# The last sum of a router layer: added by two turns into PSUM instead of by VectorE

## The chip, the cores and the metric

The kernel runs on one NeuronCore of one Trainium2 chip. The core has five engines that run side by side and wait for each other by semaphores: TensorE (PE; its weight loads are shown apart as PEld), VectorE (DVE), ScalarE (ACT), GpSimd (POOL) and SyncE (SP), which issues DMAs. The metric is device time in microseconds (us) of one execution. All arithmetic is float32.

## The reference

A small tower over 32 images of 257 tokens with 256 features. Layer 0 is a Mamba block of four scans and a mixture of experts, layer 1 is attention and a routed feed-forward. What matters here is the very last function and its last line:

```python
def _L1_ffn_ref(x, attention_mask, wr, br, w1, b1, w2, b2):
    weights = (jnp.einsum('bsd,do->bso', x, wr) + br)[..., 0]
    _, idx = jax.lax.top_k(weights, k)
    sel_idx = idx[:, :kk]
    sel = jnp.take_along_axis(x, sel_idx[:, :, None], axis=1)
    h = jax.nn.gelu(jnp.einsum('bkd,dh->bkh', sel, w1) + b1)
    y = jnp.einsum('bkh,hd->bkd', h, w2) + b2
    y = y * w_sel[..., None]
    processed = jnp.zeros_like(x).at[batch_idx, sel_idx].set(y)
    return processed + x
# layer 1, last step
h = h + _L1_ffn_ref(_layernorm(h, axis=-1), ...)
```

So the output is the sum of three terms: h, its layer norm x, and `processed`, which is y times the router's weight for a kept token and zero for the others.

## The kernel before

There are two phases with a barrier between them. `mamba_phase` does layer 0's Mamba part for all images and leaves the result in DRAM (`h_mid`). `tail_phase` does everything else. The change touches `tail_phase` alone.

`tail_phase` takes the images two at a time, in 16 groups. Features lie on the 128 partitions in two chunks (`CM = 2`), and tokens in the free dimension, so a tile such as `xh` is [128, 2 chunks, 2 images, 257 tokens]. The work of one group is cut into three stages: F (experts), A (attention) and R (router, feed-forward, output). The stages form a pipeline: in turn t, F works on group t, A on group t-1 and R on group t-2. Turns 0, 1 and 2 are written out, turns 3 to 15 are a hardware loop (waits there compare with registers), and turns 16 and 17 are written out again: turn 16 has A and R only, turn 17 has R only.

The order inside a turn is a table written by hand, `turn_order` (line 997). Each name in it is a slot: TensorE fills the PSUM banks of its stage (`ps["R"]` has two banks), another engine reads them out, and the next slot of the same stage waits for that reading by the counter `read[s]`. Each engine walks the same table, and does what it has to do in each slot. The end of the table is:

```python
A.score_1 R.hid_6 F.e1_2 R.hid_7 F.e1_3 A.turned_0 F.s2 R.y_0 F.gates_t A.turned_1 F.e2_0 R.y_1 F.e2_1 A.mix_0
F.gates_0 R.out_0 A.mix_1 R.out_1 F.gates_1
```

The slots that matter are these.

- `R.var` (line 1410): VectorE makes x, and then `xh` = x + h (line 1416).
- `R.y_0`, `R.y_1` (lines 1491 to 1499): for each chunk of features TensorE computes the second product into `ps_R` (line 1528). VectorE adds the bias and multiplies by the selected weight into `sq["R"]` (line 1495), and then adds that to `xh` (line 1499), which counts `o_ready`.
- `R.out_0`, `R.out_1` (lines 1623 to 1630): for each image TensorE turns `xh` from features on partitions to tokens on partitions. These are six transposes (three tiles of 86, 86 and 85 tokens by two chunks of features) into different columns of the two banks. ScalarE copies the result to `o_sb` (lines 1329 and 1330), and SyncE stores it with three DMAs (line 1183).
- `R.mean` of the next turn is the next user of `ps_R` after `R.out_1`.

A float32 matrix product is two MATMUL records in the trace, a transpose is one.

`sq["R"]` is written in `R.mean` by ScalarE (line 1259) and in `R.y` by VectorE. The next turn's `R.mean` stands behind `R.out_1` on TensorE.

Of the kernel before, what the change touches and what calls it, by code (L numbers as in the profile page):

```python
# [5 lines left out]
ALU = mybir.AluOpType  # L6
# [3 lines left out]
P = 128  # L10
# [5 lines left out]
CM = DM // P  # L16
# [972 lines left out]
def tail_phase(nc, a, h_mid, out):  # L989
# [26 lines left out]
    with ExitStack() as ctx:  # L1016
# [3 lines left out]
        def sem(name):  # L1020
            return ctx.enter_context(nc.semaphore(name))
# [94 lines left out]
        ahead_part = sem("ahead_part")  # L1116
        ahead_ready = sem("ahead_ready")
        xh_ready = sem("xh_ready")
        o_ready = sem("o_ready")
        stored = [sem(f"stored_{b}") for b in range(NB)]  # L1120

        n_loads = 2 * NE + 21
# [212 lines left out]
        def _(dve):  # L1335
# [62 lines left out]
            def slot(s, name, g):  # L1398
                kind, _, i = name.partition("_")
                if kind == "mean":  # L1400
                    dve.wait_ge(full[s], nth(s, name, g))
                    w = ps[s]
                    for c in range(CM):
                        last = dve.tensor_tensor(x[s][:, c, :, :], h[s][:, c, :, :], w[:, 0:NB, 0:S], ALU.subtract)
                    last.then_inc(read[s], 1)

                    dve.wait_ge(squared[s], g + 1)
                    dve.tensor_tensor(sq[s][:, 0, :, :], sq[s][:, 0, :, :], sq[s][:, 1, :, :], ALU.add
                                      ).then_inc(squares_summed[s], 1)
                elif kind == "var":  # L1410
                    norm(s, g)
                    if s == "R":

                        dve.wait_ge(x_ready[s], g + 1)
                        for c in range(CM):
                            last = dve.tensor_tensor(xh[:, c, :, :], x[s][:, c, :, :], h[s][:, c, :, :], ALU.add)
                        last.then_inc(xh_ready, 1)
                elif (s, name) == ("F", "logits"):
                    route_logits(g)
                elif (s, name) == ("F", "e1_0"):  # L1420
                    route_ranks(g)
                elif (s, name) == ("F", "e1_2"):
                    route_gates(g)
                elif (s, kind) == ("F", "gates") and i != "t":
                    dve.wait_ge(full[s], nth(s, name, g))
                    w = ps[s]
                    dve.tensor_tensor(e2[:, int(i), :, :], e2[:, int(i), :, :], w[:, 0:NB, 0:S], ALU.mult).then_inc(read[s], 1)
                elif (s, kind) == ("F", "out"):
                    c = int(i)
                    dve.wait_ge(full[s], nth(s, name, g))  # L1430
                    w = ps[s]
                    if c == 0:

                        if positive(nth("A", "mix_1", g - 1)):
                            dve.wait_ge(read["A"], nth("A", "mix_1", g - 1))
                    dve.scalar_tensor_tensor(out=h["A"][:, c, :, :], in0=w[:, 0:NB, 0:S], scalar=s_b3[:, c:c + 1],
                                             in1=h["F"][:, c, :, :], op0=ALU.add, op1=ALU.add).then_inc(read[s], 1)
                    if c == CM - 1:

                        dve.wait_ge(read[s], nth(s, name, g))  # L1440
                        sum_stream("A")
                elif (s, kind) == ("A", "score"):
                    b = int(i)
                    dve.wait_ge(full[s], nth(s, name, g))
                    w = ps[s]
                    dve.tensor_reduce(nmax[0:QT, b, 0:2], w[0:QT, 0:2, 0:S], AX.X, ALU.max, negate=True).then_inc(max_ready, 1)
                    dve.tensor_reduce(nmax[0:85, b, 2:3], w[0:85, 2, 0:S], AX.X, ALU.max, negate=True).then_inc(max_ready, 1)

                    dve.wait_ge(read[s], nth(s, name, g))
                    dve.reciprocal(precip[0:QT, b, 0:2], psums[0:QT, b, 0:2])  # L1450
                    dve.reciprocal(precip[0:85, b, 2:3], psums[0:85, b, 2:3]).then_inc(recips_ready, 1)
                    dve.wait_ge(recips_ready, g * NB + b + 1)
                    for q, (t0, n) in enumerate(TILES):
                        last = dve.tensor_scalar(prob[0:n, b, q, :], prob[0:n, b, q, :], precip[0:n, b, q:q + 1], DM ** -0.5,
                                                 ALU.mult, ALU.mult)
                    last.then_inc(probs_ready, 1)
                elif (s, kind) == ("A", "mix"):
                    b = int(i)
                    dve.wait_ge(full[s], nth(s, name, g))
                    w = ps[s]  # L1460
                    if b == 0:

                        if positive(g):
                            dve.wait_ge(xh_ready, g)
                    dve.tensor_tensor(h["R"][:, :, b, :], h["A"][:, :, b, :], w[:, 0:CM, 0:S], ALU.add).then_inc(read[s], 1)
                    if b == NB - 1:

                        dve.wait_ge(read[s], nth(s, name, g))
                        sum_stream("R")
                elif (s, name) == ("R", "hid_1"):  # L1470

                    dve.wait_ge(read[s], nth(s, "column", g))
                    for b in range(NB):
                        for t, (t0, n) in enumerate(TILES):
                            last = dve.scalar_tensor_tensor(out=ahead[0:n, b, t, :], in0=w_rows[0:n, b, :],
                                                            scalar=w_col[0:n, b, t:t + 1], in1=before[0:n, t, :],
                                                            op0=ALU.is_equal, op1=ALU.mult)
                    last.then_inc(ahead_part, 1)
                    dve.wait_ge(ahead_part, g + 1)
                    for b in range(NB):  # L1480
                        for t, (t0, n) in enumerate(TILES):
                            last = dve.scalar_tensor_tensor(out=ahead[0:n, b, t, :], in0=w_rows[0:n, b, :],
                                                            scalar=w_col[0:n, b, t:t + 1], in1=ahead[0:n, b, t, :],
                                                            op0=ALU.is_lt, op1=ALU.add)
                    last.then_inc(ahead_ready, 1)
                elif (s, name) == ("R", "rank"):
                    dve.wait_ge(full[s], nth(s, name, g))
                    w = ps[s]
                    dve.scalar_tensor_tensor(out=sel_w[:, :, :], in0=w[:, 0:NB, 0:S], scalar=float(KEPT), in1=w_rows[:, :, :],
                                             op0=ALU.is_lt, op1=ALU.mult).then_inc(read[s], 1)  # L1490
                elif (s, kind) == ("R", "y"):
                    c = int(i)
                    dve.wait_ge(full[s], nth(s, name, g))
                    w = ps[s]
                    dve.scalar_tensor_tensor(out=sq["R"][:, c, :, :], in0=w[:, 0:NB, 0:S], scalar=b_2[:, c:c + 1],  # L1495
                                             in1=sel_w[:, :, :], op0=ALU.add, op1=ALU.mult).then_inc(read[s], 1)

                    dve.wait_ge(read[s], nth(s, name, g))
                    dve.tensor_tensor(xh[:, c, :, :], xh[:, c, :, :], sq["R"][:, c, :, :], ALU.add).then_inc(o_ready, 1)

            run(dve, lambda turn: walk(turn, slot), lambda: dve.wait_ge(loaded, 16 * n_loads), lambda: None)

        @block.tensor
        def _(pe):
# [12 lines left out]
            def slot(s, name, g):  # L1517
# [86 lines left out]
                else:  # L1604
# [15 lines left out]
                    elif kind == "y":  # L1620
                        cols = slice(int(i) * P, (int(i) + 1) * P)
                        last = product(lambda b: [(w_2[:, k, cols], hid[:, k, b, :]) for k in range(HC)])
                    elif kind == "out":
                        b = int(i)
                        pe.wait_ge(o_ready, g * CM + CM)
                        flat = w[:, :, :].rearrange("p b n -> p (b n)")
                        for t, (t0, n) in enumerate(TILES):
                            for c in range(CM):
                                last = pe.matmul(flat[0:n, t * DM + c * P:t * DM + (c + 1) * P], xh[:, c, b, t0:t0 + n],  # L1629
                                                 ident[:, :], is_transpose=True, start=True, stop=True)  # L1630
                last.then_inc(full[s], 1)

            run(pe, lambda turn: walk(turn, slot), setup, lambda: None)
# [28 lines left out]
```

## Time and profile before

| | |
|---|---|
| time, median of 3 runs | 11963.23 us (11961.89 to 11964.04) |
| the profiled execution's own time | 11969.22 us |
| its span, first to last instruction | 11967.6 us |
| TensorE busy over the span | 9996.1 us, 84% |
| VectorE busy | 10589.7 us, 88% |
| ScalarE busy | 6724.8 us, 56% |
| mean granted TensorE clock | 0.921 of full speed |

The Mamba phase fills the first 10.2 ms or so of the span, and `tail_phase` the rest. Shares over the whole span say little about the second, which has limits of its own; it has to be read in its own stretch.

A row of the page's strips is 40 equal slices of the span, a digit being the busy tenths of a slice. A row of a stretch gives its length, and for each engine the busy time and the number of instructions in it, then the granted clock of TensorE as a share of full speed. A row of the timeline gives start, duration, engine, line, operation, output<-inputs, shapes and count, and in brackets how long the engine had been idle and who ended that. Neighbouring records of one kind are merged into one row; a matmul's record lasts from its issue to its modelled end, and overlaps the next one's. PEclk is 1.0 at 2.4 GHz and 0.5 at 1.2 GHz.

### The profile page before, as it was taken

What the parts mean: (1) busy time and instruction counts of PE and PEld (TensorE: products, weight loads), DVE (VectorE), ACT (ScalarE), POOL (GpSimd) and SP (SyncE); (2) the same over time, 40 slices, a digit from 0 to 9 for tenths busy, and PEclk for the clock granted to TensorE, in tenths of its full rate; (3) what the DMA queues carried; (4) which work ended last, traced back from release to release, by engine and by line L of the source; (5) the groups of instructions that cost most, each with busy time, mean ns of one, the idle gap of its engine ahead of it and who ended that gap; (6) DMA issues with size and microseconds to landing.
All of it is one profiled execution on the core that took longest, in us unless ns stands there. A gap on an engine that the chain in (4) does not pass through costs nothing. (4 is left out here: it accounts for less than half of the span.)

```text
span 11967.6 us, 119737 instructions
## 1 busy us (share of the span) xinstructions
PE 9996.1 (84%) x40728; PEld 7833.4 (65%) x40728; DVE 10589.7 (88%) x8817; ACT 6724.8 (56%) x10429; POOL 94.9 (1%) x167
## 2 busy tenths in 40 slices
PE   6888888888888888888888888888888887799998
PEld 5666666666666666666666666666666665577776
DVE  6999999999999999999999999999999999333332
ACT  5555555555656565555555555565565555244443
POOL 0000000000000000000000000000000000000000
PEclk8999999999999999999999989898999998899998
DMA  2211222222222122222221112222222111000000
GB/s 79 76 62 59 69 76 71 71 72 69 74 68 67 57 75 71 76 71 72 69 76 64 59 67 76 71 72 71 69 74 71 64 60 58 22 11 11 11 11 9
DMA packets 357681, 728.03 MB, mean 61 GB/s; under 512 B 143670, under 2 KB 188890, under 8 KB 357082
## 3 DMA queue, kind: packets, MB, share of 16 engines
q1 hardware_dynamic: 343128, 683.98, 17.1%
q0 software_dynamic: 10240, 33.56, 0.9%
q8 instruction: 328, 5.37, 0.2%
q10 hardware_dynamic: 3714, 2.89, 0.1%
q14 instruction: 271, 2.22, 0.1%
HBM read 699.27 MB, written 21.05 MB: 60 GB/s over the span
## 5 line engine op out<-in xcount | busy, mean ns | idle before, releaser
L892 PE MATMUL y_ps<-hb,ident 128*128 128x257 f32 x16384 | 4506.0, 423 | 1504.8 <-DVE hb L688 1497.9
L892 PEld LDWEIGHTS y_ps<-hb,ident 128*128 128x128 f32 x16384 | 3295.5, 208 | 2533.2 <-DVE hb L688 2022.1
L679 DVE TENSOR_TENSOR_SCAN hb<-decay,hb 128x1028 f32<-128x1028 f32 x2048 | 4722.3, 2306 | 22.4 <-issue 20.8
L505 ACT ACTIVATE decay<-delta,neg_a 128x512 f32<-128x512 f32 x4096 | 2683.0, 712 | 2194.2 <-DVE hb L679 1626.0
L688 DVE TENSOR_TENSOR hb<-hb,c_all 128x1028 f32<-128x1028 f32 x2048 | 2529.8, 1235 | 0.0
L669 DVE TENSOR_TENSOR hb<-b_all,u_buf 128x1028 f32<-128x1028 f32 x2048 | 2496.7, 1219 | 5.8
L783 PE MATMUL w_ps<-xn,in_w 128*128 128x257 f32 x4096 | 1021.8, 396 | 140.6 <-ACT xn L406 115.5
L783 PEld LDWEIGHTS w_ps<-xn,in_w 128*128 128x128 f32 x4096 | 807.7, 199 | 294.8 <-issue 129.6
L783 PE MATMUL w_ps<-xs_pad,diag_store 128*128 128x257 f32 x4096 | 954.8, 379 | 0.2
L783 PEld LDWEIGHTS w_ps<-xs_pad,diag_store 128*128 128x128 f32 x4096 | 774.2, 189 | 114.1 <-ACT diag_store L426 1.0
L783 PE MATMUL w_ps<-sz,out_w 128*128 128x257 f32 x2048 | 513.4, 395 | 0.8 <-DVE sz L696 0.8
L505 ACT ACT_TABLE_LOAD x381 | 488.8, 1283 | 6.7
L437 ACT ACTIVATE xc<-w_ps,conv_b 128x514 f32<-128x514 f32 x256 | 176.4, 689 | 551.2 <-PE w_ps L783 550.0
L783 PEld LDWEIGHTS w_ps<-sz,out_w 128*128 128x128 f32 x2048 | 413.7, 202 | 71.6 <-DVE sz L696 1.5
L783 PE MATMUL w_ps<-dtbc,dt_w 32*128 32x257 f32 x1024 | 353.5, 472 | 3.0 <-ACT cen L456 1.8
L1495 DVE SCALAR_TENSOR_TENSOR sq_R<-ps_R,b,sel_w 128x514 f32<-128x514 f32 x32 | 24.1, 753 | 352.3 <-PE ps_R L1528 352.3
L426 ACT ACTIVATE diag_store<-ident,conv_w 128x128 f32<-128x128 f32 x1024 | 323.9, 390 | 0.0
L888 PE MATMUL y_ps<-xc,skip_diag 128*128 128x257 f32 x1024 | 309.1, 429 | 7.7 <-ACT skip_diag L481 7.7
L424 ACT ACTIVATE xs_pad<-w_ps 128x514 f32<-128x514 f32 x256 | 152.6, 596 | 272.7 <-PE w_ps L783 272.6
L783 PEld LDWEIGHTS w_ps<-dtbc,dt_w 32*128 32x128 f32 x1024 | 205.8, 223 | 146.7 <-issue 117.9
L1528 PE MATMUL ps_R<-x_R,w 128*128 128x257 f32 x1024 | 274.8, 415 | 24.6 <-ACT hid L1321 22.8
L888 PEld LDWEIGHTS y_ps<-xc,skip_diag 128*128 128x128 f32 x1024 | 219.4, 219 | 71.9 <-issue 24.4
(238 smaller groups left out, 9598.5 us busy)
## 6 DMA issues: line engine op xcount, KB each, us to landing
b_all<-bc_dram SPq DMA_DIRECT2D x512, 514.0 KB, 3.6
c_all<-bc_dram SPq DMA_DIRECT2D x512, 514.0 KB, 5.0
in_w<-in_L_attn_in_w SPq DMA_DIRECT2D x64, 1024.0 KB, 5.0
x_in<-in_x POOLq DMA_DIRECT2D x128, 256.0 KB, 2.9
out_w<-in_L_attn_out_w SPq DMA_DIRECT2D x64, 512.0 KB, 3.8
h_mid<-h_cur SPq DMA_DIRECT2D x32, 257.0 KB, 3.4
h_F<-h_mid SPq DMA_DIRECT2D x16, 514.0 KB, 3.7
out<-o_sb SPq DMA_DIRECT2D x64, 86.0 KB
```

What stands on the lines that cost most here:

```text
L424: func(xs_pad[:, c % 2, :, KW - 1:], w[:, :, 0:S], ACT.Identity).then_inc(read_of(f"xs{c}", g, jj), 1)
L426: last = func(conv_diag[:, c % 2, tap, :], ident[:, :], ACT.Identity, scale=conv_w[:, k, c, tap:tap + 1])
L437: func(xc[:, jj % 2, c, :, :], w[:, :, 0:S], ACT.Silu, bias=conv_b[:, k, c:c + 1]).then_inc(read_of(f"cv{c}", g, jj), 1)
L505: last = func(decay[:, u % NDA, i, :, 1:S], delta[:, c, :, 1:S], ACT.Exp, scale=neg_a[:, k, c, NU * n + i:NU * n + i + 1])
L669: dve.tensor_tensor(hb[:, u % NHB, :, :, :].rearrange("p n b s -> p n (b s)"), b_all[:, n, :, :, :].rearrange("p n b s -> p n (b s)"), u_b ...
L679: dve.tensor_tensor_scan(h, decay[:, u % NDA, :, :, :].rearrange("p n b s -> p (n b s)"), h, 0.0, ALU.mult, ALU.add).then_inc(scan_done, 1)
L688: dve.tensor_tensor(h, h, c_all[:, u % PAIRS, :, :, :].rearrange("p n b s -> p (n b s)"), ALU.mult).then_inc(c_done, 1)
L783: last = pe.matmul(w[0:rows, b, 0:S], lhs, rhs, start=(i == 0), stop=(i == len(terms(b)) - 1))
L888: pe.matmul(y_ps[c % 2][:, b, 0:S], skip_diag[:, :], xc[:, jj % 2, c, b, :], start=True, stop=False)
L892: last = pe.matmul(y_ps[c % 2][:, b, 0:S], ident[:, :], hb[:, u % NHB, i, b, :], start=False, stop=(n == PAIRS - 1 and i == NU - 1))
L1495: dve.scalar_tensor_tensor(out=sq["R"][:, c, :, :], in0=w[:, 0:NB, 0:S], scalar=b_2[:, c:c + 1], in1=sel_w[:, :, :], op0=ALU.add, op1=ALU. ...
L1528: last = pe.matmul(w[rows, b, 0:S], lhs, rhs, start=(k == 0), stop=(k == len(terms(b)) - 1))
```

## The change

VectorE no longer adds `sq["R"]` to `xh` in the two `R.y` slots. TensorE instead turns both tiles, each into the same columns of PSUM: the first transpose starts the columns (`start`), the second adds to them (`stop`). So each `R.out` slot has twelve transposes where it had six. TensorE waits for `xh_ready` and for the reading of `y_1` in place of `o_ready`, and that semaphore is gone. Lines below line 1119 move up by one, and later ones by two to four.

```diff
-        o_ready = sem("o_ready")
...
                     dve.scalar_tensor_tensor(out=sq["R"][:, c, :, :], in0=w[:, 0:NB, 0:S], scalar=b_2[:, c:c + 1],
                                              in1=sel_w[:, :, :], op0=ALU.add, op1=ALU.mult).then_inc(read[s], 1)
-
-                    dve.wait_ge(read[s], nth(s, name, g))
-                    dve.tensor_tensor(xh[:, c, :, :], xh[:, c, :, :], sq["R"][:, c, :, :], ALU.add).then_inc(o_ready, 1)
...
                     elif kind == "out":
                         b = int(i)
-                        pe.wait_ge(o_ready, g * CM + CM)
+                        pe.wait_ge(xh_ready, g + 1)
+                        pe.wait_ge(read[s], nth(s, "y_1", g))
                         flat = w[:, :, :].rearrange("p b n -> p (b n)")
                         for t, (t0, n) in enumerate(TILES):
                             for c in range(CM):
-                                last = pe.matmul(flat[0:n, t * DM + c * P:t * DM + (c + 1) * P], xh[:, c, b, t0:t0 + n],
-                                                 ident[:, :], is_transpose=True, start=True, stop=True)
+                                for k, part in enumerate((xh, sq["R"])):
+                                    last = pe.matmul(flat[0:n, t * DM + c * P:t * DM + (c + 1) * P], part[:, c, b, t0:t0 + n],
+                                                     ident[:, :], is_transpose=True, start=(k == 0), stop=(k == 1))
```

On TensorE, in the loop's turn, this stood at `R.out_0` before (`ident` is the unit matrix, `ps_A<-prob_t,value` is `A.mix_1`; a row with x3 stands for three instructions, and brackets name the semaphores waited for):

```order
L1523 REGISTER_ALU
L1625 ISA [waits read_R]
L1629 MATMUL ps_R<-ident,xh 86x128 [waits o_ready]
L1629 MATMUL ps_R<-ident,xh 86x128 x3
L1629 MATMUL ps_R<-ident,xh 85x128 x2
L1523 REGISTER_ALU
L1602 MATMUL ps_A<-prob_t,value 128x257 [waits read_A]
```

and this stands there now:

```order
L1627 MATMUL ps_R<-ident,xh 86x128 [waits read_R,xh_ready]
L1627 MATMUL ps_R<-ident,sq_R 86x128
L1627 MATMUL ps_R<-ident,xh 86x128
L1627 MATMUL ps_R<-ident,sq_R 86x128
L1627 MATMUL ps_R<-ident,xh 86x128
L1627 MATMUL ps_R<-ident,sq_R 86x128
L1627 MATMUL ps_R<-ident,xh 86x128
L1627 MATMUL ps_R<-ident,sq_R 86x128
L1627 MATMUL ps_R<-ident,xh 85x128
L1627 MATMUL ps_R<-ident,sq_R 85x128
L1627 MATMUL ps_R<-ident,xh 85x128
L1627 MATMUL ps_R<-ident,sq_R 85x128
```

Twelve transposes stand where six did, and the separate waiting instruction ahead of them is gone; the slots ahead and behind are the same.

On VectorE, in the same turn, the two `R.y` slots were these (`ps_R` is the product, `h_R` belongs to `A.mix_0`):

```order
L1495 SCALAR_TENSOR_TENSOR sq_R<-ps_R,b,sel_w 128x514 [waits full_R]
L1499 TENSOR_TENSOR xh<-xh,sq_R 128x514 [waits read_R]
L1493 REGISTER_ALU
L1495 SCALAR_TENSOR_TENSOR sq_R<-ps_R,b,sel_w 128x514 [waits full_R]
L1499 TENSOR_TENSOR xh<-xh,sq_R 128x514 [waits read_R]
L1459 REGISTER_ALU
L1465 TENSOR_TENSOR h_R<-h_A,ps_A 128x2x257 [waits xh_ready,full_A]
```

and are these now:

```order
L1494 SCALAR_TENSOR_TENSOR sq_R<-ps_R,b,sel_w 128x514 [waits full_R]
L1492 REGISTER_ALU
L1494 SCALAR_TENSOR_TENSOR sq_R<-ps_R,b,sel_w 128x514 [waits full_R]
L1458 REGISTER_ALU
L1464 TENSOR_TENSOR h_R<-h_A,ps_A 128x2x257 [waits xh_ready,full_A]
```

The two additions are gone, and nothing else on VectorE has moved.

## Rows read from the trace of the kernel before

**Rows 1.** The page's strips: busy tenths in 40 slices.

```profile
PE   6888888888888888888888888888888887799998
DVE  6999999999999999999999999999999999333332
```

**Rows 2.** Stretches, from R.mean to R.mean: turns 2 to 15; then turns 12, 11, 14.

```profile
10391.73:11799.88 1408.15, 1327.09 (x6273) 1029.03 (x6273) 453.46 (x1022) 697.87 (x1078) 15.33 (x14) 0.97 0.04 10
11396.31:11495.76 99.45, 93.92 (x449) 72.75 (x449) 32.41 (x73) 49.88 (x77) 1.09 (x1) 0.98 0.04 11
11295.35:11396.31 100.96, 93.92 (x449) 72.76 (x449) 32.38 (x73) 49.91 (x77) 1.09 (x1) 0.98 0.04 10
11595.57:11697.81 102.24, 97.21 (x449) 75.41 (x449) 32.42 (x73) 49.91 (x77) 1.10 (x1) 0.95 0.03 10
```

**Rows 3.** Waits of TensorE behind VectorE's addition: the total, times, the longest.

```profile
PE ps_R L1629 <- DVE xh L1499: 1.7, 1, 1.7
```

**Rows 4.** Timeline of one turn of the loop around R.out_0 and R.out_1.

```profile
11387.11 0.69 DVE L1499 TENSOR_TENSOR xh<-xh,sq_R 128x514 f32<-128x514 f32 x1
...
11391.10 0.85 PE L1629 MATMUL ps_R<-ident,xh 128*86 128x128 f32 x6
...
11391.80 2.77 PE L1602 MATMUL ps_A<-prob_t,value 86*128 86x257 f32 x12
...
11394.41 0.82 PE L1629 MATMUL ps_R<-ident,xh 128*86 128x128 f32 x6
...
11395.16 1.13 PE L1528 MATMUL ps_F<-gate_t,pair_rows 4*128 4x257 f32 x4
...
11395.33 0.70 DVE L1344 TENSOR_TENSOR rstd_R<-h_R 128x514 f32<-128x514 f32 x1
11395.75 0.37 ACT L1330 ACTIVATE o_sb<-ps_R 85x256 f32<-85x256 f32 x1
...
11396.26 1.13 PE L1528 MATMUL ps_R<-rstd_R,mean_w 128*128 128x257 f32 x4
```

**Rows 5.** One line's instructions, nanoseconds min/median/max: the transposes, the addition.

```profile
L1629 PE MATMUL ps_R<-ident,xh x192: 270/273/311, 10487.6 to 11956.6; 128*86 128x128 f32 x128, 128*85 128x128 f32 x64
```

```profile
L1499 DVE TENSOR_TENSOR xh<-xh,sq_R x32: 694/695/697, 10474.0 to 11953.4; 128x514 f32<-128x514 f32 x32
```

**Rows 6.** Timeline of turn 16, which has no gates slots.

```profile
11878.44 0.82 PE L1629 MATMUL ps_R<-ident,xh 128*86 128x128 f32 x6
...
11879.38 2.87 PE L1602 MATMUL ps_A<-prob_t,value 86*128 86x257 f32 x12
...
11883.87 1.14 PE L1528 MATMUL ps_R<-rstd_R,mean_w 128*128 128x257 f32 x4 [0.95 <-ACT o_sb L1330]
```

**Rows 7.** Timeline of the end of turn 17.

```profile
11952.59 0.75 DVE L1495 SCALAR_TENSOR_TENSOR sq_R<-ps_R,b,sel_w 128x514 f32<-128x514 f32 x1 [6.57 <-PE ps_R L1528]
11953.38 0.69 DVE L1499 TENSOR_TENSOR xh<-xh,sq_R 128x514 f32<-128x514 f32 x1
...
11954.22 0.83 PE L1629 MATMUL ps_R<-ident,xh 128*86 128x128 f32 x6 [1.67 <-DVE xh L1499]
...
11955.98 4.98 SPq L1183 DMA_DIRECT2D out<-o_sb  x6
...
11957.39 0.37 ACT L1330 ACTIVATE o_sb<-ps_R 85x256 f32<-85x256 f32 x1
```

**Rows 8.** Timeline of TensorE in turn 17: one form of block at two clocks.

```profile
11910.74 3.79 PE L1528 MATMUL ps_R<-x_R,w 128*128 128x257 f32 x8 [0.78 <-ACT hid L1321]
...
11934.52 2.00 PE L1528 MATMUL ps_R<-x_R,w 128*128 128x257 f32 x8 [0.78 <-ACT hid L1321]
```

**Rows 9.** A stretch with fifteen transposes in it, and the stretch that holds R.column.

```profile
11375.70:11382.00 6.30, 6.30 (x41) 4.92 (x40) 1.45 (x2) 2.15 (x4) 0.00 (x0) 1.00 0.00 0
```

```profile
11416.10:11420.80 4.70, 4.70 (x21) 3.94 (x22) 0.69 (x1) 4.48 (x7) 0.00 (x0) 0.64 0.00 0
```

**Rows 10.** R.column on TensorE, at the start of the second of these stretches.

```profile
11416.09 1.07 PE L1613 MATMUL ps_R<-ones,w_row 1*86 1x1 f32 x12 [1.37 <-ACT hid L1321]
```

## The prediction

> **What bounds the kernel now.** First the page's strips [rows 1]. In the first 33 slices VectorE is at nine tenths and TensorE at eight: that is the Mamba phase, which the change doesn't touch. In the slices that follow it is the other way round, TensorE at seven to nine tenths and VectorE at three, and there the changed code runs. The view of stretches confirms it [rows 2]: turns 2 to 15 take 1408.15 us, in which TensorE is busy for 1327.09 (94%) and VectorE for 453.46 (32%). So the change takes work from an engine that is idle two thirds of the time and gives it to the one that sets the pace.
>
> Next, who waits for the removed addition. The table of waits has one wait of TensorE behind it in the whole phase, 1.7 us [rows 3]. The timeline of a turn of the loop shows why [rows 4]: the addition for `y_1` starts at 11387.11 and lasts 0.69, so it is done at 11387.80, and TensorE reaches `R.out_0` at 11391.10. The addition had 3.3 us of slack, with `A.mix_0` and `F.gates_0` as its cover. Nothing of VectorE's waits in its shadow either: its next instruction waits for `A.mix_0`. So in the loop the removal is worth nothing.
>
> **The cost of a transpose.** The trace has 192 of them, 270 to 311 ns each, median 273 [rows 5], but they overlap, so what counts is the spacing of their starts. `R.out_1`'s block of six is 0.82 us long [rows 4]; less the last one's 0.273 that leaves 0.547 us for five steps, 0.109 us each. `R.out_0`'s block gives (0.85 - 0.273) / 5 = 0.115, since its first step is a little longer; the added ones come behind the first. I take 0.109. As a check, `R.out_0` starts at 11391.10 and `A.mix_1` at 11391.80, 0.70 us for six. The added transposes have the same shapes and the same moving operand, and a stationary one of the same size. What the trace doesn't show is a transpose that adds to PSUM. Bounds for one: 0 from below, if it hid wholly under its neighbour's load, which no row shows; from above 0.217, a step of the neighbouring float32 products (`A.mix_1`, twelve in 11391.80 to 11394.41), were it done as two passes like them. The shapes decide for 0.109.
>
> The Trainium skill, "TensorE: Matmul & The Clock Gate", section "Back-to-back issue gap", gives N/2.4 + 2.5 ns for a single stream at full clock, which is 56 ns for 128 columns; the page's example is bf16. The rows here have twice that for float32, and the measurement decides. By the page's figure the added 192 would cost 10.7 us rather than 20.9.
>
> **The sum at an unchanged clock.**
> - Turns 2 to 15: twelve more transposes each, 12 x 0.109 = 1.31 us. Does anything absorb it? Behind `R.out_0` comes `A.mix_1` without a pause, behind `R.out_1` comes `F.gates_1` without a pause. The next turn's `R.mean` starts at 11396.26, when the last ScalarE copy of `R.out_1` (11395.75 + 0.37 = 11396.12) is done; VectorE's `rstd_R` was there at 11396.03 [rows 4]. The copy moves with the transposes, so that wait stays, and at most 0.1 us a turn is won if it was VectorE's. ScalarE's copy of `R.out_0` has to be done before `R.out_1`; it has the 2.6 us of `A.mix_1` for that, and the added steps shift both alike. 14 x 1.31 = 18.3 us.
> - Turn 16: from `R.out_0` (11878.44) to `A.mix_1` (11879.38) are 0.94 us where six transposes need 0.70; `A.mix_1` waits for VectorE there [rows 6]. So 0.25 of the added 0.65 is hidden, +0.40. `R.mean` then waits for the copy of `R.out_1`, so the other six count in full, +0.65. Together +1.05.
> - Turn 17: here the removal is worth something. TensorE waits for `y_1`'s reading and then for the addition, from 11953.38 to 11954.22 [rows 7]. That goes, about -0.75; late next is the reading itself, done at 11953.34. `R.out_0`'s six added steps (+0.65) make its copy 0.1 us earlier than before. `R.out_1` comes 0.55 later, but its three stores stand in SyncE's queue, which issues six in 4.98 us, 0.83 each: the fourth is due at 11955.98 + 2.49 = 11958.47, and the copy that it needs was done at 11957.39 + 0.37 = 11957.76, now 11958.31. So the end moves by -0.1, at worst by +0.55.
>
> 18.3 + 1.05 - 0.1 = +19.3 us.
>
> **The clock term.** The 14 turns do the same work and don't take the same time. Three kinds stand in the rows [rows 2]: 99.45, 100.96 and 102.24 us. Seven of the 14 are near the first (99.7 in the mean), four near the second (101.0), three near the third (102.1), and the mean of all is 1408.15 / 14 = 100.58. TensorE's own busy time is 93.9 in the first two and 97.2 in the third. The difference is where a stretch at 1.2 GHz falls. The usual place is behind a thin piece, a wait of 1.37 us and the twelve tiny matmuls of `R.column` [rows 10], in a stretch whose granted clock is 0.64 [rows 9]. The cheap kind is half of all turns before. A turn that is 1.31 us longer meets the clock at another point each time, and there is no reason for it to keep the cheap half; I expect the middle kind, 101.0 of before's time. 14 x (101.0 - 100.58) = +5.9 us. Bounds: all cheap, 14 x (99.7 - 100.58) = -12.3; all dear, 14 x (102.1 - 100.58) = +21.3. In turn 17 a block of eight takes 2.00 us at 2.4 GHz and 3.79 at 1.2 [rows 8]; one or two blocks may change sides, +-3.6.
>
> **The total.** The profiled execution had 11969.22 us, 1.6 more than its span of 11967.6, and 6.0 more than the median of 11963.23. Its sum is 11969.2 + 19.3 + 5.9 = 11994.4; against the median 11963.2 + 25.2 = 11988.4, rounded to 11988. A measurement of this kernel tells about 0.2% from no change, 23.9 us, so the line between slower and no change is at 11987.2, right under the forecast.
>
> **The rivals.**
> - *The cheap turns stay as many.* Then only the steady sum is left: 11963.2 + 19.3 = 11982.5, no change. For it: the sequence of turns repeats itself over long stretches, and could do so again. Against: it repeats with a length that the change alters.
> - *Not slower: the stretch at 1.2 GHz always falls cheaply.* The place is `R.column` and the slots behind it. If the longer turn put it there every time, all turns would be 99.7 + 1.3, and the sum 19.3 - 12.3 = +7.0, 11970.2. It decides from a mean turn below 102.2 us (100.58 + 1.31 + 0.33); under that the whole is within 0.2%. Half of before's turns speak for it, the change of phase against it.
> - *Transposes don't hold the clock.* `R.out` with its neighbours now has 24 transposes in 6 us. If the clock fell there, each turn would get a second stretch at half clock, and be of the dear kind: 14 x 1.5 = +21.3 over the mean of before, 11963.2 + 19.3 + 21.3 = 12003.8. Against it: `F.gates_t` and `A.turned_1`, 15 transposes in a row, stand in a stretch with a granted clock of 1.00, and the products behind them too [rows 9]. The same time comes out if the stretches of before just fall at dear places.
> - *The adding transpose takes two passes,* 0.217 in place of 0.109. +20.9 more in 192, 11963.2 + 25.2 + 20.9 = 12009.3. Nothing in the trace speaks for it but the products.
> - *Faster: the freed VectorE lets TensorE go on.* Price: all the waits behind the addition, 1.7 us [rows 3], against 19.3. I don't see it.
>
> The Trainium skill, the same page, section "Part 4: PE-mode transpose", states that transposing doesn't count as TensorE activity for the clock in the way that products do. That is the third rival's rule. By it the sum would be the 12003.8 of that rival; what this case's rows have against it is the 1.00 beside fifteen transposes, which are fewer and shorter together than what comes now.
>
> **How the numbers follow.** The forecast with its clock term has 0.56, with a range of its own from 11984 to 11994; about two thirds of that, 0.38, is over 11987.2. The first rival has 0.20, the second 0.08, the third 0.10, the fourth 0.04, the last 0.02. Slower: 0.38 + 0.10 + 0.04 = 0.52. No change: 0.18 + 0.20 + 0.08 = 0.46. Faster: 0.02. The range from 11977 to 12002 holds the forecast and the first rival whole and what lies halfway to the second and the third; it leaves out about 0.2.
>
> **What would show it.** In the profile after: 384 transposes with a median of 273 ns, blocks of twelve about 1.47 us long, `A.mix_1` 1.35 us behind `R.out_0` and `F.gates_1` 1.40 behind `R.out_1`; no line for the addition, VectorE's busy time in turns 2 to 15 lower by 28 x 0.695 = 19.5 us with no wait of TensorE gone; turns with a mean of 102.3 us, and of the kinds 100.8, 102.3 and 103.5; the last copy of turn 17 at 0.55 later, the end unmoved. A spacing above 0.109, a mean turn below 102.2, or a granted clock under 1.00 around `R.out` would make the forecast wrong, each in its own way.

## The result and the profile after

| | before | changed |
|---|---|---|
| median of 15 runs | 11965.38 us (11958.32 to 11977.47) | 11993.11 us (11982.17 to 12005.43) |
| ratio | | 1.0021, 95% interval 1.0013 to 1.0029 |
| profiled execution, its own time | 11969.22 us | 11994.06 us |
| span | 11967.6 us | 11992.5 us |

The change makes the kernel slower by 0.21%, 25 us, with an interval from 16 to 35; the two medians are 27.7 us apart. The forecast of 11988 against 11963.2 was +24.8, and the profiled span grew by 24.9. More executions of the kernel before moved its median to 11965.4.

The changed kernel's stretches, from R.mean to R.mean, columns as in [rows 2] (turns 2 to 15 together; turns 2, 6 and 12; then turns 16 and 17 from another view):

```profile
10390.08:11825.05 1434.97, 1341.07 (x6440) 1042.98 (x6441) 433.94 (x994) 698.46 (x1078) 15.37 (x14) 0.98 0.03 10
10390.08:10494.01 103.93, 96.80 (x461) 75.04 (x461) 30.79 (x71) 49.89 (x77) 1.10 (x1) 0.97 0.03 7
...
10800.91:10904.45 103.54, 98.52 (x462) 76.66 (x461) 31.04 (x71) 49.93 (x77) 1.10 (x1) 0.95 0.03 10
...
11415.95:11518.24 102.29, 95.23 (x462) 74.08 (x461) 31.01 (x71) 49.91 (x77) 1.10 (x1) 0.98 0.03 10
```

```profile
11825.00:11910.79 85.79, 76.25 (x343) 59.27 (x342) 24.03 (x48) 34.13 (x56) 0.00 (x0) 0.94 0.02 7
11910.79:11992.50 81.71, 52.41 (x196) 37.08 (x196) 11.72 (x22) 15.09 (x23) 0.00 (x0) 0.76 0.04 11
```

Turns 2 to 15 took 1408.15 and now take 1434.97 us. Turns 16 and 17 before were these:

```profile
11799.88:11883.91 84.03, 74.65 (x332) 57.58 (x331) 25.42 (x50) 34.12 (x56) 0.00 (x0) 0.94 0.03 8
11883.91:11967.60 83.69, 53.16 (x184) 36.99 (x184) 13.10 (x24) 15.07 (x23) 0.00 (x0) 0.73 0.04 11
```

In turns 2 to 15 VectorE's busy time fell by 19.5 us, and nothing came of it. TensorE has 12 instructions more a turn (461 where it had 449). And the mix of [rows 2] is gone: 12 of the 14 turns last 102.24 to 102.35 us.

The transposes, minimum/median/maximum in ns:

```profile
L1627 PE MATMUL ps_R<-ident,xh x192: 271/273/311, 10487.5 to 11982.0; 128*86 128x128 f32 x128, 128*85 128x128 f32 x64
...
L1627 PE MATMUL ps_R<-ident,sq_R x192: 270/273/273, 10487.7 to 11982.1; 128*86 128x128 f32 x128, 128*85 128x128 f32 x64
```

Those that add to PSUM (`sq_R`) are as long as those that start the columns. TensorE's timeline in `R.out_0` of a loop turn gives their spacing:

```profile
11409.48 0.31 PE L1627 MATMUL ps_R<-ident,xh 128*86 128x128 f32 x1
11409.63 0.27 PE L1627 MATMUL ps_R<-ident,sq_R 128*86 128x128 f32 x1
11409.74 0.27 PE L1627 MATMUL ps_R<-ident,xh 128*86 128x128 f32 x1
...
11410.72 0.27 PE L1627 MATMUL ps_R<-ident,sq_R 128*85 128x128 f32 x1
11410.83 1.03 PE L1598 MATMUL ps_A<-prob_t,value 86*128 86x257 f32 x4
```

Steps of 0.109 us, and `A.mix_1` starts 1.35 us behind the first transpose, where it was 0.70 in [rows 4]. The stretch around the transposes has a granted clock of 1.00:

```profile
11408.00:11417.00 9.00, 9.00 (x52) 7.15 (x51) 3.46 (x5) 1.73 (x4) 0.00 (x0) 1.00 0.09 25
```

Where the clock does fall shows in TensorE's timeline of turn 12. In the kernel before (99.45 us) it falls in the blocks behind `R.column` (the twelve matmuls of [rows 10]), and `F.logits` (L1551, 24 matmuls with four columns each) and the block behind it run at full clock:

```profile
11417.09 1.79 PE L1528 MATMUL ps_A<-sq_A,mean_w 128*128 128x257 f32 x4
11418.67 2.97 PE L1528 MATMUL ps_R<-x_R,w 128*128 128x257 f32 x8
...
11423.03 1.97 PE L1528 MATMUL ps_A<-x_A,qk_t 128*128 128x257 f32 x8 [0.52 <-DVE x_A L1339]
...
11443.13 2.74 PE L1551 MATMUL ps_F<-g_w,x_F 128*128 128x4 f32 x24
11445.73 1.98 PE L1528 MATMUL ps_R<-x_R,w 128*128 128x257 f32 x8
```

In the changed kernel (102.29 us) it is the other way round: full clock behind `R.column`, half clock behind `F.logits` (now L1547):

```profile
11436.78 1.14 PE L1524 MATMUL ps_A<-sq_A,mean_w 128*128 128x257 f32 x4
11437.75 1.90 PE L1524 MATMUL ps_R<-x_R,w 128*128 128x257 f32 x8
...
11442.55 1.97 PE L1524 MATMUL ps_A<-x_A,qk_t 128*128 128x257 f32 x8 [2.03 <-DVE x_A L1338]
```

```profile
11462.65 2.74 PE L1547 MATMUL ps_F<-g_w,x_F 128*128 128x4 f32 x24
11465.25 3.12 PE L1524 MATMUL ps_R<-x_R,w 128*128 128x257 f32 x8
11468.16 2.49 PE L1524 MATMUL ps_F<-x_F,e_w 128*128 128x257 f32 x8
```

Before, the blocks behind `R.column` ran at half clock (2.97 us for a block of eight matmul records, 1.90 at full clock). In the changed kernel they run at full clock, and yet `A.key_0` (output `ps_A`, input `qk_t`) starts hardly sooner: 11423.03 - 11396.31 = 26.72 us into the turn before, 11442.55 - 11415.95 = 26.60 now. It waits for VectorE's x_A, 0.52 us before and 2.03 now. So half clock at this place costs 0.1 us: it fills a wait. Behind `F.logits` TensorE waits for nobody, and half clock costs its full price. That place is what the turn of 102.29 us pays for, and the prediction had not seen it.

The trace of the kernel before had it too. In its turn 11, of the middle kind (100.96 us), the one stretch at half clock stands behind `F.logits`:

```profile
11341.99 2.74 PE L1551 MATMUL ps_F<-g_w,x_F 128*128 128x4 f32 x24
11344.59 2.66 PE L1528 MATMUL ps_R<-x_R,w 128*128 128x257 f32 x8
11347.05 2.94 PE L1528 MATMUL ps_F<-x_F,e_w 128*128 128x257 f32 x8
```

By the granted clock of the trace, the seven turns of the cheap kind have no such stretch behind `F.logits`, the four of the middle kind and the three of the dear kind have one, and the dear ones have a long one at `R.column` besides. In the changed kernel all 14 turns have it behind `F.logits`.

### The profile page after: what moved, and what is told of

Read it like the earlier page. It is cut to its first block and busy times, and to the rows that moved or that the text cites. A ratio compares the mean times of both kernels' runs of the same rounds, so it can differ in the third digit from the quotient of the medians.

```text
span 11992.5 us, 120089 instructions
## 1 busy us (share of the span) xinstructions
PE 10023.3 (84%) x40920; PEld 7860.6 (66%) x40920; DVE 10567.8 (88%) x8785; ACT 6726.6 (56%) x10429; POOL 95.2 (1%) x167
## 5 line engine op out<-in xcount | busy, mean ns | idle before, releaser
L1524 PE MATMUL ps_R<-x_R,w 128*128 128x257 f32 x1024 | 273.6, 414 | 24.7 <-ACT hid L1320 22.9
```

The costliest lines, as they stand in the source:

```text
L1524: last = pe.matmul(w[rows, b, 0:S], lhs, rhs, start=(k == 0), stop=(k == len(terms(b)) - 1))
```

## The experiments

All times are beside runs of the kernel before on the same chip, ratios with their 95% intervals. An interval is about 0.09% wide to either side, 11 us. In the profile I read turns 2 to 15, where a single execution shows every turn.

**The removal alone.** From the changed kernel:

```diff
-                                for k, part in enumerate((xh, sq["R"])):
+                                for k, part in enumerate((xh,)):
-                                                     ident[:, :], is_transpose=True, start=(k == 0), stop=(k == 1))
+                                                     ident[:, :], is_transpose=True, start=True, stop=True)
```

> The changed kernel with six transposes of xh in each R.out slot and no transposes of sq_R, and without VectorE's addition: the term processed is left out of the output. This is the removal alone. Theory (the sum was hidden in the loop): turns 2 to 15 as before, 1408 us in the profile give or take 15 for where the half clock falls, no wait of TensorE gone but the 1.7 us of turn 17; time within 0.1% of before, at most 1 us less from its own doing. Rival (the freed VectorE lets TensorE go on): the cheap turns become shorter than 99.4 us, and the time falls by 5 us or more.

Measured: ratio 0.9998 (0.9989 to 1.0007), turns 2 to 15 in 1414.71 us. The cheapest turn is 99.33 us, against 99.45 before. That is under the 99.4 of the rival, but the addition's removal is not what made it: a kernel below that keeps the addition has turns of 99.27. The median didn't fall by 5 us (11965.89 against 11965.34), though the interval, 13 us less to 8 more, doesn't exclude that by itself. What excludes it is the table of waits: in turns 2 to 15 it has no wait of TensorE behind the addition in the kernel before, so there was none to remove. The total is 6.6 us over that of [rows 2] with the same work on TensorE, which says how much one execution's mix of turns can differ from another's.

**The transposes alone.** From the kernel before, VectorE's addition kept:

```diff
-                                last = pe.matmul(flat[0:n, ...], xh[:, c, b, t0:t0 + n], ident[:, :], is_transpose=True, start=True, stop=True)
+                                for k in range(2):
+                                    last = pe.matmul(flat[0:n, ...], xh[:, c, b, t0:t0 + n], ident[:, :], is_transpose=True, start=True, stop=True)
```

> The kernel before, with VectorE's addition kept, and each transpose of xh in R.out issued twice, the second overwriting the first: the added twelve transposes alone, and none of them adds in PSUM. Theory (the cost is twelve more transposes a turn, and adding in PSUM costs nothing): spacing 0.109 us, turns of 102.29 us nearly all through as in the changed kernel, turns 2 to 15 in 1433 to 1436 us, time as the changed kernel's, 0.15 to 0.27% over before. Rival (adding in PSUM, or alternating two source tiles, costs something of its own): cheaper than the changed kernel by that.

Measured: 1.0020 (1.0011 to 1.0029), 1433.75 us, 13 of 14 turns within 102.24 to 102.42. That is the changed kernel's result without a single transpose that adds, and with VectorE's additions still there. All of the loss is in the number of transposes.

**Another twelve.** From the changed kernel (each xh turned twice, its first result overwritten):

```diff
-                                for k, part in enumerate((xh, sq["R"])):
+                                for k, part in enumerate((xh, xh, sq["R"])):
-                                                     ... start=(k == 0), stop=(k == 1))
+                                                     ... start=(k <= 1), stop=(k != 1))
```

> The changed kernel with a third transpose for each pair: xh is turned twice (the first is overwritten) and sq_R added, so 24 transposes more than before in a turn in place of twelve. Linear theory: a cheap turn is 99.45 + 2.62 = 102.1 us, the kinds 102.3, 103.6, 104.8. Theory of the clock's place: with twelve the turns came to 102.29, the middle kind, nearly always; with 24 the sequence changes again and all three kinds come back, so the mean turn is 103.0 to 104.0, and the step from twelve to 24 is between 0.5 and 1.5 us a turn rather than the 1.92 us that the step from none to twelve cost. Rival (every added transpose costs 0.16 us, whatever the clock): 100.58 + 3.84 = 104.4 us.

Measured: 1.0026 (1.0016 to 1.0036), 1438.40 us. The mean turn is 102.74 us, so the step from twelve to 24 is about 0.3 us a turn where the transposes alone are 1.31. It fell even below the range that I gave. In nine of its turns the half clock falls at `R.column` alone, and these are the cheap kind again (101.98 to 102.36); the other five (103.59 to 104.27) have it behind `F.logits`. One of each:

```profile
11106.90:11208.88 101.98, 96.55 (x474) 75.39 (x473) 31.03 (x71) 49.82 (x77) 1.09 (x1) 0.98 0.04 10
11208.88:11312.68 103.80, 98.22 (x474) 76.67 (x473) 31.02 (x71) 49.82 (x77) 1.10 (x1) 0.97 0.04 10
```

**Half the dose.** From the kernel before, the second image's transposes of `xh` issued twice, `for k in range(1 + b)`:

> The kernel before with six transposes more in a turn rather than twelve (R.out_1's of xh issued twice, VectorE's addition kept). Linear theory: 14 x 0.65 = 9 us more, mean turn 101.2, time 0.08% over before. Theory of the clock's place: the turn's length decides where the stretches at half clock fall, in jumps, so half of the transposes doesn't cost half; with 0.65 us more the long stretches of the dear kind should be frequent, mean turn 101.5 to 102.4, time 0.11 to 0.2% over before.

Measured: 1.0013 (1.0004 to 1.0022), 1433.08 us. Half the transposes cost as much in the profile as all of them did, because all 14 turns have the half clock behind `F.logits`, and ten of them a long stretch at `R.column` too, which makes them the dear kind. One of these and one of the other four:

```profile
10906.96:11009.77 102.81, 97.78 (x456) 75.95 (x455) 32.42 (x73) 49.91 (x77) 1.09 (x1) 0.95 0.04 10
11009.77:11111.39 101.62, 94.58 (x456) 73.42 (x455) 32.40 (x73) 49.84 (x77) 1.09 (x1) 0.98 0.03 10
```

The profiled execution is the slowest of this kernel's 11 (11997.71 us, median 11987.56), so its share of dear turns is high for it; the timed ratio, between the linear 1.0008 and the full dose's 1.0021, agrees with both theories by its interval (1.0004 to 1.0022). That half the dose costs as much as the whole is shown for this one execution, not for the kernel.

**F.logits with wider matmuls, on the changed kernel.** The small weights `g_w` are read 16 times over as the moving operand, and only the first four columns are used:

```diff
-                dve.tensor_tensor(lg[:, :, :], w[:, 0, 0:6 * NE].rearrange("p (t e) -> p t e", e=NE),
+                dve.tensor_tensor(lg[:, :, :], w[:, 0, 0:6 * 64].rearrange("p (t e) -> p t e", e=64)[:, :, 0:NE],
-                                last = pe.matmul(w[:, 0, NE * t:NE * (t + 1)], xs[:, c, b, t0:t0 + P], g_w[:, c, :],
+                                last = pe.matmul(w[:, 0, 64 * t:64 * (t + 1)].rearrange("p (r e) -> p r e", e=NE), xs[:, c, b, t0:t0 + P],
+                                                 g_w[:, c, :].unsqueeze(1).to_broadcast([P, 16, NE]),
```

> The changed kernel with F.logits' 24 tiny matmuls made wider: the moving operand g_w is read 16 times over, so each writes 64 columns rather than 4 and only the first four are read. In the changed kernel the half clock falls right behind F.logits in 13 of 14 turns. Theory (the thin matmuls of F.logits are what lets the clock fall there, at the price of 1.3 us a turn): F.logits stays near 2.6 us, the stretch at half clock behind it is gone from most turns, the mean turn falls from 102.5 to 100.5 to 101.5, and the time by 10 to 25 us. Rival (the clock falls there for some other reason, or it just falls later): mean turn within 0.3 us of 102.5, or more by what 24 wider matmuls take.

Measured: 1.0000 (0.9991 to 1.0009) against the kernel before, 11965.84 us: the whole loss of the change is made good, by an edit elsewhere that adds work. Turns 2 to 15 take 1413.81 us. Two neighbouring turns, one without any half clock and one with it at `R.column`:

```profile
11188.81:11289.50 100.69, 93.55 (x461) 72.89 (x461) 31.02 (x71) 49.82 (x77) 1.10 (x1) 1.00 0.04 10
11289.50:11390.21 100.71, 95.23 (x461) 74.07 (x461) 31.04 (x71) 49.81 (x77) 1.09 (x1) 0.98 0.04 10
```

They are equally long, though TensorE is busy 1.68 us longer in the second. So a short stretch at half clock behind `R.column` is free. It isn't when it begins in `R.column` itself, as in two other turns of this kernel (101.15 and 101.26 us): that costs 0.5. A longer one there costs about 1 us: the turns of 100.23 and 100.40 in the next kernel. A turn of the changed kernel with it behind `F.logits` has 102.29, so there it costs 1.6 us. The block itself and the one behind it, in TensorE's timeline of this kernel:

```profile
11436.92 2.79 PE L1547 MATMUL ps_F<-g_w,x_F 128*128 128x64 f32 x24
11439.54 1.95 PE L1524 MATMUL ps_R<-x_R,w 128*128 128x257 f32 x8
```

2.62 us from start to start with 64 columns, 2.60 with four: the width is free. Behind it the products take 1.95 where they took 3.12. No turn of this kernel has half clock behind `F.logits`; in the changed kernel it was all 14 (the expectation says 13). So the narrow matmuls are what let the clock fall there.

**The same on the kernel before.** The edit is the same.

> The kernel before with the wider matmuls of F.logits (64 columns written rather than 4, the first four read). In the changed kernel this made turns of 100.6 to 100.7 us wherever no long stretch at half clock fell, with or without one at R.column: so the half clock costs 1.6 us behind F.logits and nothing at R.column, where TensorE waits for x_A afterwards in any case. Theory: turns of 99.3 to 99.9 here, the kind of 101.0 gone, turns 2 to 15 in 1391 to 1402 us (1408 before), time 5 to 20 us under before. Rival (the wider matmuls help only where the clock always fell there, and the cheap half of before's turns was already as good): mean turn 100.4 or more, time within 4 us of before.

Measured: 0.9979 (0.9970 to 0.9988), 11944.89 us. This is faster than both kernels. Its turns 2 to 15 and a turn that never left full clock:

```profile
10387.70:11781.29 1393.59, 1314.24 (x6272) 1018.98 (x6273) 453.36 (x1022) 697.87 (x1078) 15.35 (x14) 0.98 0.04 10
...
11483.42:11582.71 99.29, 92.24 (x449) 71.58 (x449) 32.42 (x73) 49.86 (x77) 1.10 (x1) 1.00 0.04 11
```

Twelve turns are within 99.27 to 99.75, two are 100.23 and 100.40; the kind of 101.0 is gone. Against the changed kernel with the same edit, 1413.81, the change costs 20.2 us here, 1.44 a turn, near the bare 1.31. Turn 2 has 3.0 of these 20.2 us (102.33 against 99.29): in the changed kernel's execution it begins at half clock, in the other it has none; the other 13 differ by 1.32 each. With the costly place of the clock removed, the change is what its transposes are. (The timed ratios, 1.0000 and 0.9979, are 25 us apart, too coarse to tell 18 from 25.)

**R.column behind A.var, on TensorE alone.** From the changed kernel:

```diff
+        pe_order = list(order)
+        pe_order.remove(("R", "column", 2))
+        pe_order.insert(pe_order.index(("A", "var", 1)) + 1, ("R", "column", 2))
```

> The changed kernel with TensorE's R.column behind A.var rather than ahead of it (on TensorE alone; the other engines keep their order). A.var's input is ready before the hid_0 reading that R.column waits for. Theory (TensorE's weak place is a chain: R.column's wait for ScalarE delays A.var, that delays x_A, and A.key_0 waits for it): the wait for x_A, 23.7 us in the changed kernel, shrinks to under 12 or moves, the turn of 102.29 becomes 101.2 to 101.8, the time 7 to 15 us less. Rival (ScalarE's table loads and its own order set that time): x_A comes no sooner, the time within 4 us of the changed kernel, or R.hid_1 is late and it is slower.

Measured: 1.0017 (1.0008 to 1.0026), against 1.0021: no gain that can be told. 13 of 14 turns are still within 102.23 to 102.47. `A.var` comes earlier, but not what hangs on it:

```profile
11539.17 1.11 PE L1528 MATMUL ps_A<-sq_A,mean_w 128*128 128x257 f32 x4
...
11543.06 0.69 ACT L1254 ACTIVATE rstd_A<-ps_A,eps_t 128x514 f32<-128x514 f32 x1
...
11545.73 1.30 DVE L1342 TENSOR_TENSOR x_A<-x_A,rstd_A 128x514 f32<-128x514 f32 x2 [3.36 <-ACT rstd_A L1257]
```

The turn began at 11520.53, so x_A starts 25.20 us into it; in the changed kernel it is 11441.10 - 11415.95 = 25.15. ScalarE reads `A.var` at its own time: `A.var`'s block is over at 11540.28, and ScalarE does sq_F, the two column copies and a table load before it comes to it at 11543.06. The rival was right, and TensorE's wait for x_A grew, from 24.7 to 35.0 us in turns 2 to 15.

**Both places widened and the order changed, on the kernel before.** The two diffs together, and R.column at 64 columns (of which the first is read):

```diff
-                                last = pe.matmul(w[0:n, b, t:t + 1], w_row[:, b, t0:t0 + n], ones[0:1, 0:1], start=True, stop=True)
+                                last = pe.matmul(w[0:n, b, 64 * t:64 * (t + 1)], w_row[:, b, t0:t0 + n], ones[0:1, 0:64], start=True, stop=True)
```

> The kernel before with three edits: F.logits at 64 columns, R.column at 64 columns rather than 1, and R.column behind A.var on TensorE. If both places are what the clock falls at and the chain at R.column is worth 0.5 to 1 us: turns of 98.3 to 99.0 us, turns 2 to 15 in 1376 to 1390 us, time 20 to 35 us under before (0.17 to 0.3%). If only F.logits counts: as the kernel with the wide F.logits alone.

Measured: 0.9981 (0.9972 to 0.9990), 11945.64 us: as the wide `F.logits` alone, so only that one counts, and the turns of 98.3 to 99.0 that the first theory wanted didn't come. Turns 2 to 15 take 1391.11 us, and all 14 last 99.29 to 99.56, whether their granted clock is 1.00 or 0.98. In these turns waits set the time, not the clock:

```profile
11405.84 3.66 PE L1533 MATMUL ps_A<-x_A,qk_t 128*128 128x257 f32 x8 [2.50 <-DVE x_A L1344]
```

Here `A.key_0` itself runs at half clock, behind the wait for x_A (3.66 us, 1.97 at full clock), and the turn has 99.37 us all the same. A second wait, ahead of `A.key_1` for ScalarE's copy of the keys, takes it up but for 0.2 us (`A.key_1` starts 31.90 us into this turn and 31.66 into one without half clock), and the slot behind that the rest.

**Repeats for the size of the clock term.** These are the kernel before twice more and the changed one once, with nothing changed in what they do. Each is a single execution.

> The kernel before once more, for the size of the clock term. The profiled executions so far have 1408.15 us in turns 2 to 15 for the kernel before, and 1414.72 for the one without the sum, which has the same work on TensorE. Theory (in the kernel before the three kinds of turn mix as it happens, and one execution is a draw): 1404 to 1418 us, another mix of 99.3 to 99.9, 101.0 and 101.6 to 102.3. Rival (before settles into the same cheap sequence each time): within 2 us of 1408, seven cheap turns again.

> As the run ahead of it, a further execution: 1404 to 1418 us by the theory of a draw, within 2 us of 1408 by the rival.

> The changed kernel once more. Its profiled execution had 1434.97 us in turns 2 to 15, and the kernel with each transpose issued twice 1433.76. Theory (a turn of 102.29 us holds its own place, with the half clock behind F.logits each time): 1432 to 1437 us, ten or more of the 14 turns within 102.2 to 102.5. Rival (a draw like before's): 1425 to 1440 us, with turns of 100.8 us among them. If the theories of both kernels hold, the clock term is the mean difference less 18.3 us.

Measured: 1413.91 and 1410.65 us for the kernel before, 1432.35 for the changed one, all 14 of whose turns are within 102.24 to 102.43. Before varies from one execution to the next, as the theory of a draw has it, and the changed kernel keeps its turn. The first execution of before, 1408.15, was its lowest. By the number of added transposes in a turn, all profiled executions without the wide `F.logits` or the other order, and beside them how many of the 14 turns have half clock behind `F.logits`, and what the timed medians gained over before's:

| added a turn | turns 2 to 15, us | mean | over none | transposes alone | turns with half clock behind F.logits (of these with a long stretch at R.column) | timed medians, over before |
|---|---|---|---|---|---|---|
| 0 | 1408.15, 1414.71, 1413.91, 1410.65 | 1411.9 | | | 7 (3), 9 (7), 9 (6), 8 (4) | |
| 6 | 1433.08 | | 21.2 | 9.2 | 14 (10) | 18.4 |
| 12 | 1434.97, 1433.75, 1432.35 | 1433.7 | 21.8 | 18.3 | 14 (1), 14 (1), 14 (0) | 27.7, 26.5 |
| 24 | 1438.40 | | 26.5 | 36.6 | 5 (0) | 31.6 |

(The second execution of the first row is the removal alone, which has the same work on TensorE.) Each row has its own random part, 3 us or so either way where none is added, and the rows of 6 and 24 are one execution each. In the profile the curve is no line: the first six cost most of what 24 do. The timed runs don't show this by themselves, since their intervals (5 to 26, 16 to 35 and 19 to 43 us) hold the transposes alone, 9, 18 and 37, as well. What carries it is the count of turns. An estimate from it, with the 1.6 us of a stretch behind `F.logits` and the 1.0 of a long one at `R.column`: the average execution without added transposes has 8.25 of the first and 5 of the second. Twelve transposes make that 14 and 0.7, +4.9 us where 21.8 - 18.3 = +3.5 were measured; six make it 14 and 10, +14.2 for 12.0 measured; 24 make it 5 and none, -10.2 for -10.1 measured. For the twelve of the change the clock's part is 21.8 - 18.3 = 3.5 us in the profiles, and 27.7 less the steady 19.3, 8.4 us, in the timed medians, which can be 10 us off.

## Why the prediction was right

- **The removal is worth nothing in the loop.** Right; 0.9998 for the removal alone, and no wait of TensorE behind the addition in turns 2 to 15. That answers the last rival as well. VectorE's 19.5 us were saved where nobody waited.
- **0.109 us a transpose, adding or not.** Right to the third digit; the Trainium skill's formula ("TensorE: Matmul & The Clock Gate", "Back-to-back issue gap") would have halved it, and no run here supports that for float32 transposes. The prediction took the section's formula for products without weight loads; for pairs of a load and a product with 128 columns the same section has about 81 ns, and the 109 here are over that too.
- **18.3 us in turns 2 to 15.** The spacing and the starts of the next slots are as foretold, and the two kernels with a wide `F.logits` differ by 20.2, or 1.32 a turn from turn 3 on.
- **Turn 16, +1.05.** Measured 85.79 - 84.03 = +1.76, of which the change has +0.92: from `R.out_0` to the next `R.mean` there were 11883.87 - 11878.44 = 5.43 us, and now 11910.84 - 11904.49 = 6.35. `R.out_0` to `A.mix_1` grew by 0.37 (0.94 to 1.31), where 0.40 was said. The other 0.8 us is there before `R.out_0`, where TensorE has the same work: the stretches at half clock fall at other points. The twelve matmuls of `R.column` alone took 1.44 us before and 1.90 in the changed kernel, 0.5 of the 0.8.
- **Turn 17.** Its end kept its place behind the last reading, between the -0.1 and the +0.55 that were said. From the end of `y_1`'s reading (11953.34, [rows 7]) to the end of the span there were 14.26 us, and in the changed kernel, 11978.24 to 11992.5, it is 14.26 again. The turn as a whole got 2.0 us shorter, with a granted clock of 0.76 where it was 0.73; the prediction had put +-3.6 on that. The time before turn 2 became 1.6 us shorter (R.mean at 10390.08, not 10391.73), but the repeats of the kernel before have 10381.45 and 10391.33 there, so that is chance. The four pieces together, 26.8 + 1.8 - 2.0 - 1.7, are the 24.9 of the span. That this meets the forecast's +24.8 so closely is luck: the last two took away 3.6 us that the forecast didn't have, and the loop and turn 16 had 3.3 more than it gave.
- **The clock term, +5.9.** In the one pair that the forecast is about it is 26.8 - 18.3 = +8.5; in the means of the table +3.5. The forecast lies between the two, and its reason was half wrong, so the size is in part luck. It was right that a turn of another length doesn't keep before's cheap half. It was wrong about the place: the step "the difference is where a stretch at 1.2 GHz falls; the usual place is behind a thin piece ... `R.column`" names a place where a short stretch costs nothing (100.69 against 100.71). The price is paid behind `F.logits`. And I expected kinds of 100.8, 102.3 and 103.5 us that average to the middle one, where 12 of 14 turns are the middle one and none is of 100.8. It was luck, too, to count from 1408.15: from before's mean of 1411.9 the same reasoning, 14 x 101.0, gives +2.1.
- **The first rival, as many cheap turns,** is out by its mechanism: none of the 28 turns of the changed kernel's two executions is without half clock behind `F.logits`, where before had about six of 14. Its time is not: its +19.3 lies within the measured 16 to 35.
- **The second rival, always cheap,** is out here, since the dear place took every turn. It is what the wide `F.logits` brings about: the time is 11965.84, and nine of 14 turns have 100.56 to 100.71.
- **The third rival, transposes that don't hold the clock,** is out: 24 of them with their neighbours stand in a stretch at 1.00, and in none of the turns 2 to 15 does half clock fall there. The rule of the Trainium skill ("TensorE: Matmul & The Clock Gate", "Part 4: PE-mode transpose") isn't contradicted as such, since products surround them, but it had no effect here.
- **The fourth rival, two passes,** is out by the count of records, 384, and by the steps of 0.109 us. The rows gave it less than the prediction said: the 0.217 us of its price is the step of one record with 257 columns, and 0.109 of one with 128, so the products take no second pass per record that a transpose might share.

The line between slower and no change was set at 11987.2, right under the forecast. The measured ratio's lower end, 1.0013, shows how near it was: that it is slower is shown, that it is more than 0.2% is not.

## What to carry to other kernels

Work moved onto the engine that sets the pace cost its whole length here, though the work removed elsewhere was longer: in turns 2 to 15, 28 additions of 0.695 us bought nothing, and 168 transposes at 0.109 us each cost 18 us, some 22 with the clock. Look for the wait behind a removed instruction before counting its duration. And where equal turns of a loop have unequal lengths, find which stretches at half clock cost something before a percent is fought for: here a short stretch in front of a wait was free and one in a dense run cost 1.6 us, and widening 24 tiny matmuls, which took no longer for it, gained as much as the change under study lost.

## What the runs showed of the hardware that I had not expected

- A float32 matmul with 64 moving columns behind a load of 128 takes as long as one with four: 24 in 2.62 us against 2.60. Behind the narrow ones the granted clock fell to half in all of the changed kernel's turns 2 to 15 and in seven of before's 14, behind the wide ones in none, in either kernel.
- Transposes that add in PSUM cost no more than those that start the columns: a step of 0.109 us in both.
- Turns of a loop can be fixed or wander by their length. With twelve transposes more, 39 of 42 turns in three executions are 102.24 to 102.43 us, while without them the same loop wanders between 99.3 and 102.3. Why it does is not shown.
- So the cost of work need not be proportional to it at this scale: six, twelve and 24 transposes more in a turn cost 21, 22 and 27 us in the profile, with one execution each for six and 24.
